# Softplus in a state-space layer: the predicated copy and VectorE's part in it taken out, the two branches added up by ScalarE and GpSimd

## What is computed

```python
xz = hidden_states @ in_proj_w.T
x, z = jnp.split(xz, 2, axis=-1)
x = silu(causal convolution of x with 4 taps)
dt, Bm, C = jnp.split(x @ x_proj_w.T, [16, 32], axis=-1)
dt = jax.nn.softplus(dt @ dt_proj_w.T + dt_proj_b)
def step(h, ins):
    dA = jnp.exp(dt_t[:, :, None] * A)
    h = dA * h + dt_t[:, :, None] * B_t[:, None, :] * x_t[:, :, None]
    y = jnp.einsum('bdn,bn->bd', h, C_t)
y = ys + x * D
return y * silu(z) @ out_proj_w.T
```

## Time and profile before

| | |
|---|---|
| Median of 3 runs | 3272.32 us (3270.14 to 3275.8) |
| Profiled execution, its own time | 3271.81 us |
| Its span, first to last instruction | 3270.1 us |
| Last stage | from about 2190 us to the end |
| DVE busy in 2190 to 3270 us | 977.99 us |
| PE, POOL, ACT busy in the same stretch | 946.28, 858.00, 509.88 us |

### The profile page before, as it was taken

The page is one execution under the profiler, slowest core; times in us unless marked ns, Lnnn a source line. Parts: engine busy times, 40 slices in busy tenths (PEclk is TensorE's granted clock), DMA queues, the critical chain, the costliest instruction groups (busy, mean ns, idle before and its releaser), DMA issues.

```text
span 3270.1 us, 45199 instructions
## 1 busy us (share of the span) xinstructions
PE 2865.6 (88%) x14018; PEld 1320.2 (40%) x14055; DVE 2167.0 (66%) x3006; ACT 1420.8 (43%) x2463; POOL 1267.8 (39%) x1424
## 2 busy tenths in 40 slices
PE   6895798988988989869999999678899899999986
PEld 5662133333332333236666666563222233223222
DVE  3577876866866767022222222564999999999997
ACT  2341055655655656812122211435445445545442
POOL 1143012112212212210000000744888888898885
PEclk9997588988999989979999999888899999998978
DMA  6166413133132220041111111740000000000000
GB/s 206 52 213 161 152 28 61 28 59 55 34 58 38 51 48 24 19 135 32 32 30 32 32 31 26 224 152 7 1 14 20 1 20 20 1 20 14 1 13 20
DMA packets 175061, 176.60 MB, mean 54 GB/s; under 512 B 50674, under 2 KB 151541, under 8 KB 174749
## 3 DMA queue, kind: packets, MB, share of 16 engines
q1 hardware_dynamic: 168732, 157.52, 18.9%
q0 software_dynamic: 6144, 16.82, 1.6%
HBM read 100.46 MB, written 73.83 MB: 53 GB/s over the span
## 4 chain that ended last, share of the span: by engine, by line
PE 54%; DVE 18%; POOL 10%; issue 9%; ACT 4%; DMA 3%; SPq 1%; POOLq 0%; DVEq 0%; ACTq 0%; PEldq 0%
PE ps L1679 50%; DVE hh L1645 6%; DVE mp L1421 6%; POOL Ch L907 5%; DVE ps L1632 2%; PE ps L1887 2%; POOL yg L806 2%; DMA ks<-qk_parts 1%; ACT Pt L1029 1%; DVE tl L1622 1%; DVE q L1333 1%; SPq L529 1%; PE ps L1843 1%; SPq L620 1%; ACT dA L1209 1%
## 5 line engine op out<-in xcount | busy, mean ns | idle before, releaser
L1421 DVE TENSOR_REDUCE mp<-ps 128x1 f32<-128x1024 f32 (+7 forms) x768 | 669.4, 909 | 245.3 <-PE ps L1679 234.2
L1029 ACT ACTIVATE Pt<-ps 128x512 f32<-128x512 f32 (+3 forms) x1280 | 609.2, 539 | 477.3 <-PE ps L1679 472.2
L907 POOL TENSOR_TENSOR Ch<-hh,Cb 128x1024 f32<-128x1024 f32 x256 | 603.1, 2358 | 41.0 <-DVE hh L1645 41.0
L1679 PE MATMUL ps<-ks,qs 96*128 96x512 bf16 (+3 forms) x1280 | 392.0, 379 | 96.2 <-DVE mp L1421 48.6
L1645 DVE TENSOR_TENSOR_SCAN hh<-dA,hst,ps 128x512 f32<-128x512 f32 x384 | 472.8, 1262 | 0.0
L767 POOL TENSOR_SCALAR_AFFINE_SELECT Pt<-Pt 128x128 f32<-128x128 f32 x512 | 146.8, 292 | 837.1 <-ACT Pt L1029 828.6
L1679 PE MATMUL ps<-qs,ks 99*128 99x512 bf16 (+3 forms) x1280 | 406.9, 365 | 16.0 <-ACT Pt L1029 15.6
L1209 ACT ACTIVATE dA<-ps 128x1024 f32<-128x1024 f32 x256 | 261.8, 1023 | 356.2 <-PE ps L1679 355.8
L1679 PE MATMUL ps<-dtx,pick 32*128 32x512 f32 x1024 | 324.8, 685 | 74.0 <-DVE hh L1645 73.1
L1632 DVE TENSOR_TENSOR ps<-ps,Bb 128x512 f32<-128x512 f32 x512 | 325.4, 680 | 28.0 <-PE ps L1679 27.7
L1679 PE MATMUL ps<-dt,WA 32*128 32x512 f32 x1024 | 321.1, 706 | 15.6 <-ACT dA L1209 14.6
(11 more groups left out here) (303 smaller groups left out, 3770.5 us busy)
## 6 DMA issues: line engine op xcount, KB each, us to landing
W<-in_L_ffn_w SPq DMA_DIRECT2D x16, 1024.0 KB, 12.1
qk_parts<-q SPq DMA_DIRECT2D x32, 384.0 KB, 2.9
qs<-qk_parts SPq DMA_DIRECT2D x96, 128.0 KB, 6.1
ks<-qk_parts SPq DMA_DIRECT2D x96, 128.0 KB, 7.8
expert_out<-yb SPq DMA_DIRECT2D x72, 128.5 KB, 2.6
...
```

The lines of the kernel that those rows point to most:

```text
L907: pool.tensor_tensor(Ch[:, k % 6, :, :], hh[:, k % HRING, :, :], Cb[:, par:par + 1, :].broadcast_to([P, 2, CH]), ALU.mult).then_inc(s_Ch, 1)
L1029: act.activation(Pt[:, n % PRING, q0:CH], ps[:, 4 + n % SRING, q0:CH], ACT.Exp, scale=SCALE).then_inc(s_exp, 1)
L1421: dve.tensor_reduce(mp[:, qc, h, t % TPC, k0 // 1024:k0 // 1024 + 1], slot[:, 0:n], AX.X, ALU.max).then_inc(s_free, 1)
L1679: return pe.matmul(o, lhsT, rhs, start=start, stop=stop, **kw)
```

## The change

Softplus' logarithm and its series are no longer chosen between; they are added. With a turning point t = 6 ln 2, ScalarE makes two exponentials: e1 = exp(-min(|v|, t)) (through a Relu of t - |v|), and e2 = exp(-max(|v|, t)) (through a Relu of |v| - t). The one that does not apply stays at the constant 2^-6. The result is max(v, 0) + ln(1 + e1) - ln(1 + 2^-6) + e2 * q(e2), where q is a quadratic that ScalarE makes with Square and Identity; `fix` holds the constants. For a block, ACT issues ten instructions where it issued five, POOL four where it issued six, and DVE none where it issued one. PE's queue is the same, instruction for instruction.

The function `series` and the functions `mask` and `select` are gone; `below_above` and `logarithm` are ACT's new ones, and `step_size` is POOL's, now in two steps.

```diff
-            def series(m, d, step):
...
-                    po.link(pool.tensor_scalar(p, t, 1.0 / 3, -0.5, ALU.mult, ALU.add))
-                    po.mark(pool.tensor_tensor(p, p, t, ALU.mult))
...
-                    po.link(pool.tensor_scalar(p, p, 1.0, 1.0, ALU.mult, ALU.add))
-                    pool.tensor_tensor(p, p, t, ALU.mult).then_inc(s_poly, 1)
...
-                pool.wait_ge(s_sel, b)
-                pool.tensor_tensor(dt[:, par, d, :], dt[:, par, d, :], tl[:, d, :], ALU.add).then_inc(s_dt, 1)
...
+            def step_size(m, d, step):
+
+                par, b = m % 2, m * KI + d + 1
+                x, q = dt[:, par, d, :], dtx[:, par, d, :]
                 if step == 0:
+                    pool.wait_ge(s_ln, b)
+                    po.mark(pool.tensor_tensor(x, x, tl[:, d, :], ALU.add))
+                    po.mark(pool.tensor_tensor(q, q, te[:, d, :], ALU.mult))
                 if step == 1:
                     po.settle()
+                    pool.tensor_tensor(x, x, q, ALU.add).then_inc(s_dt, 1)
+                    pool.wait_ge(s_dt, b)
+                    pool.wait_ge(s_xs, m + 1)
+                    pool.tensor_tensor(q, x, xs[:, par, d, :], ALU.mult).then_inc(s_dtx, 1)
...
-                if n == 0 and u in (5, 9, 13):
-                    step_size(0, u // 4)
-                if n + 1 < NC and u == 28:
-                    step_size(n + 1, 0)
-                if n and u in (0, 4, 8):
-                    step_size(n, u // 4 + 1)
...
+                if n == 0 and u in (2, 3, 7, 9, 13, 15):
+                    step_size(0, 1 + u // 6, u in (3, 9, 15))
                 if n + 1 < NC and u in (23, 25, 27, 29):
-                    series(n + 1, (u - 23) // 4, (u - 23) // 2 % 2)
-                if n + 1 < NC and u == 31:
-                    series(n + 1, 2, 0)
-                if n and u in (1, 3, 5):
-                    series(n, (2, 3, 3)[u // 2], (1, 0, 1)[u // 2])
+                    step_size(n + 1, (u - 23) // 4, (u - 23) // 2 % 2)
+                if n and u in (0, 4, 7, 9):
+                    step_size(n, 2 + u // 6, u in (4, 9))
...
                 ac.settle()
-                ac.link(act.activation(te[:, d, :], te[:, d, :], ACT.Exp, scale=-1.0))
-                act.activation(tl[:, d, :], te[:, d, :], ACT.Ln, bias=1.0).then_inc(s_ln, 1)
...
+            def below_above(m, d):
+
+                t, l = te[:, d, :], tl[:, d, :]
+                ac.mark(act.activation(l, t, ACT.Relu, bias=fix[:, 0:1], scale=-1.0))
+                ac.settle()
+                ac.mark(act.activation(t, t, ACT.Relu, bias=fix[:, 1:2]))
+                ac.settle()
+                ac.mark(act.activation(l, l, ACT.Exp, bias=fix[:, 1:2]))
+                ac.mark(act.activation(t, t, ACT.Exp, bias=fix[:, 1:2], scale=-1.0))
+                ac.settle()
+
+            def logarithm(m, d):
...
+                ac.mark(act.activation(l, l, ACT.Ln, bias=1.0))
+                ac.mark(act.activation(q, t, ACT.Square, bias=fix[:, 2:3], scale=1.0 / math.sqrt(3.0)))
+                ac.settle()
+                ac.mark(act.activation(l, l, ACT.Identity, bias=fix[:, 5:6]))
+                ac.mark(act.activation(q, q, ACT.Identity, bias=fix[:, 3:4]))
+                ac.settle()
+                act.sem_inc(s_ln, 1)
...
             take_BC(0, 1)
+            below_above(0, 0)
+            logarithm(0, 0)
             for d in range(1, KI):
                 take_dt(0, d)
-            mask(0, 0)
...
-                if n == 0 and u in (3, 7, 11):
-                    mask(0, u // 4 + 1)
-                if n and u in (2, 6):
-                    mask(n, u // 4 + 2)
+                if n == 0 and u in (0, 4, 7):
+                    below_above(0, (0, 4, 7).index(u) + 1)
+                if n == 0 and u in (1, 5, 9):
+                    logarithm(0, (1, 5, 9).index(u) + 1)
+                if n and u == 3:
+                    below_above(n, 3)
+                if n and u == 5:
+                    logarithm(n, 3)
...
-                if u in (26, 30):
-                    mask(n + 1, u // 4 - 6)
+                if u in (20, 24, 27):
+                    below_above(n + 1, (20, 24, 27).index(u))
+                if u in (21, 26, 29):
+                    logarithm(n + 1, (21, 26, 29).index(u))
...
-                dve.wait_ge(s_mask, m * KI + d + 1)
-                dve.copy_predicated(tl[:, d, :], te[:, d, :].bitcast(I32), dtx[:, m % 2, d, :]).then_inc(s_sel, 1)
...
-                if n == 0 and u in (5, 9, 13):
-                    select(0, u // 4)
-                if n + 1 < NC and u == 28:
-                    select(n + 1, 0)
-                if n and u in (0, 4, 8):
-                    select(n, u // 4 + 1)
```

More of the change, by code:

```diff
@@ L1132, in _ @@
             act.activation(A[:, :, :], A[:, :, :], ACT.Exp).then_inc(s_expA, 1)
+            act.wait_ge(s_none, 3)
+            ac.link(act.activation(fix[:, 6:7], fix[:, 4:5], ACT.Exp, bias=fix[:, 1:2]))
+            ac.link(act.activation(fix[:, 7:8], fix[:, 6:7], ACT.Ln, bias=1.0))
+            ac.link(act.activation(fix[:, 5:6], fix[:, 7:8], ACT.Copy, scale=-1.0))
             def take_x(m, d):
```

32 lines of the change are left out of this document (11 added, 21 removed).

## The result

The changed kernel took 3284.61 us in the median of six runs (3277.3 to 3289.16), the kernel before 3271.36 us on the same chip (3267.2 to 3275.8, six runs). The ratio is 1.0039, with a 95% interval of 1.0028 to 1.0049. I had forecast 3262 us and a range up to 3279. The profiled execution took 3277.3 us, its span 3275.5 us. It is the shortest of its six, but its last stage is 11.0 us longer than before, 1092.5 us against 1081.5.

The account below looks back on a forecast made before the run. DVE was taken as nearest to full in the last stage, with the dense chunk borders deciding. Borders 9.5, start -3.0 and chunk 0 3.6 gave 10 us off 3271.8; median forecast 3262 us, own range 3256 to 3267, with rivals 3240 to 3279.

Parts of the forecast that it names:

- The selects' price: At the seven chunk borders: removing DVE's selects wins 28.5 us if ACT is in time.
- ACT's groups: ACT's new instructions per block: `below_above` takes 2.82 us, `logarithm` 2.62, a dependent instruction 0.74.
- rival (4): Units 27 to 31: ACT becomes the bound if dependent instructions cost 0.2 us more; 3279 us, chance 0.15.
- rival 5: Last stage: POOL still ends last, so only select and series time on its chain goes, 5 us; 3267, chance 0.05.
- Step (c): Border 3/4 behind z3: a fixed sequence gives units 4 and 5 their spreads 10.7 and 15.0 us later; nothing won yet.
- Step (b): Border 3/4, units 27 to 31: ACT's groups delay PE 1.3 us, then half a microsecond; z3 ends 2.2 us later.
- Step (a): Border 3/4, from unit 20: ACT's groups put PE 2 us behind, won back in units 24 to 26, 0.6 behind at 27.
- the walk's delay for ACT: All seven borders: ACT's added work takes 19.0 us off the gain of 28.5, leaving 9.5.
- My own sign of being wrong: Borders 3/4 and 4/5: the prediction is wrong if they win more than 5 us or nothing.
- the last of the chances: Clock stretches falling elsewhere add a few microseconds to either side, within the range 3240 to 3279.
- Start: Start of the last stage: block 0's ACT groups ahead of the dt copies make z0 and the first spread 3.0 us later.
- Chunk 0: Chunk 0's three selects cost 0.8, 2.6 and 2.5 us; ACT's first group delays PE 2.3; 3.6 won.

Follow-up runs that it names:

- run 2: The kernel before with its 32 selects left out and nothing else changed: 0.9898 of the kernel before.
- run 8: The changed kernel with only block 0's ACT groups cut into pairs, in units 21 to 24, and some POOL steps moved: 1.0023 of the kernel before.
- run 9: The changed kernel with only blocks 1 to 3's ACT groups in pairs and later places, block 0's left: 0.9981 of the kernel before.
- run 4: The changed kernel with the spread of dt*x issued twice in units 22 and 23: 0.998 of the kernel before.
- run 6: The kernel before with the spread of dt*x issued twice in unit 22: 0.9984 of the kernel before.
- run 10: The changed kernel with the spread of dt*x issued twice in units 12 and 18 instead: 1.004 of the kernel before.
- run 12: The kernel before, unchanged, run once more for its trace: 3322.73 us, one execution.
- run 7: run 3 with repeated spreads in units 18 and 22, chunk 0's groups in pairs, and the start's groups behind the dt copies: 0.9925 of the kernel before.
- run 11: run 3 with the spread repeated in unit 22 and the start's ACT groups behind the dt copies: 0.9891 of the kernel before, 3283.54 us.
- second pair: One more execution each of the kernel before and the changed kernel, both unaltered, on other chips: last stage 1082.1 and 1095.3 us.
- run 3: The changed kernel with ACT's groups at the borders cut into pairs or moved to later units, POOL's steps behind them: 0.9935 of the kernel before.

## Why the prediction was wrong

**What held.** The selects' price as a sum: 28.5 us at the borders, 27.0 measured. ACT's groups: 2.82 and 2.62 us forecast, 2717.94 - 2715.06 = 2.88 and 2722.12 - 2719.34 = 2.78 in these rows of ACT in the changed kernel, with 0.75 us from one dependent instruction to the next where I took 0.74:

```profile
2715.06 0.73 ACT L1168 ACTIVATE tl<-te,fix 128x512 f32<-128x512 f32 x1
2715.82 0.72 ACT L1170 ACTIVATE te<-te,fix 128x512 f32<-128x512 f32 x1
2716.57 0.72 ACT L1172 ACTIVATE tl<-tl,fix 128x512 f32<-128x512 f32 x1
2717.20 0.71 ACT L1173 ACTIVATE te<-te,fix 128x512 f32<-128x512 f32 x1
2717.94 1.02 ACT L1217 ACTIVATE dA<-ps 128x1024 f32<-128x1024 f32 x1
...
2719.34 0.63 ACT L1181 ACTIVATE tl<-tl 128x512 f32<-128x512 f32 x1
...
2721.24 0.71 ACT L1185 ACTIVATE dtx<-dtx,fix 128x512 f32<-128x512 f32 x1
2722.12 1.02 ACT L1217 ACTIVATE dA<-ps 128x1024 f32<-128x1024 f32 x1 [0.17 <-ACT dtx L1185]
```

So rival (4) did not come about by its own condition, a dearer dependent instruction, although the result is on its side. POOL did not set the pace (rival 5): at every border its `Ch` of unit 0 starts 0.2 us or less behind DVE's unit, where before it was 3.2 to 7.1.

**Step (c), the fixed sequence behind z3, held to 0.1 us.** In the changed kernel z3 is made in the first row here:

```profile
2761.63 1.98 PE L1682 MATMUL ps<-xin,inw 128*128 128x512 f32 x4
...
2773.22 1.02 PE L1682 MATMUL ps<-dtx,pick 32*128 32x512 f32 x4
...
2778.01 0.59 PE L1682 MATMUL ps<-dtx,pick 32*128 32x512 f32 x2
```

It ends at 2763.61. The spreads for units 4 and 5 end at 2774.24 and 2778.60, 10.6 and 15.0 us later; the step said 10.7 and 15.0. DVE stands ready for both, and waits 1.53 and 0.84 us:

```profile
2774.29 1.30 DVE L1642 TENSOR_TENSOR ps<-ps,Bb 128x512 f32<-128x512 f32 x2 [1.53 <-PE ps L1682]
2775.50 2.32 DVE L1655 TENSOR_TENSOR_SCAN hh<-dA,ps 128x512 f32<-128x512 f32 x2
2778.66 1.30 DVE L1642 TENSOR_TENSOR ps<-ps,Bb 128x512 f32<-128x512 f32 x2 [0.84 <-PE ps L1682]
```

These waits are not ACT's doing alone: run 2, without its groups, has them too.

**Step (b) held in its sum, not in its parts.** PE's z3 ends 7.7 us behind DVE's unit 31 with the groups and 5.6 without (runs 8 and 9), 2.1 later where the step had 2.2. Units 0 to 8 show the same: ACT's groups cost 262.1 - 247.7 = 14.4 us there over all borders (run 4 against run 2), 2.06 a border. But the group in unit 27 makes PE wait 0.52 us in its unit 29 (run 4, at full clock, in the rows below), where the step had 1.3 a unit earlier.

**Step (a) failed.** It said that PE would be 2 us behind in unit 23, "wins it back in units 24 to 26, 0.6 behind at 27". The late spread came where it was forecast. But I costed units 24 to 26 at the full-clock pace of PE, in a stretch where the change had just put gaps of 0.48, 0.32 and 1.12 us in place of one of 1.56. The clock went to 1.2 GHz among them, PE won nothing back, and units 24 to 31 of the seven borders cost 244.9 - 216.2 = 29 us over run 2, where step (a) gives some 4 (7 x 0.6). With the repeats of run 4 they cost 219.9 - 216.2 = 3.7, and the borders are then 8.9 us better than before (482.0 against 490.9), where I had 9.5.

The step also left a group out. Block 1's `below_above` stands in unit 24, ahead of the `decay` that PE's unit 26 waits for, and the walk has no wait there. Run 4 shows it where units 24 to 31 have no half clock, at border 5/6: PE in its units 26 and 29, and DVE's `drive` of unit 30, up to whose spread PE does not idle again.

```profile
3031.66 1.13 PE L1682 MATMUL ps<-dt,WA 32*128 32x512 f32 x4 [1.31 <-ACT dA L1217]
...
3044.43 1.13 PE L1682 MATMUL ps<-dt,WA 32*128 32x512 f32 x4 [0.52 <-ACT dA L1217]
```

```profile
3040.97 1.30 DVE L1642 TENSOR_TENSOR ps<-ps,Bb 128x512 f32<-128x512 f32 x2 [1.17 <-PE ps L1682]
```

The wait of 1.3 us in unit 26 is there at six of run 4's seven borders.

That 8.9 comes so close to 9.5 flatters me. Run 4 has less half clock at its borders (54.4 us) than run 2 (92.7) and the kernel before (97.0), and the kernel before wins 9.5 us at its borders as well when it gets its own repeat (run 6, 481.4). With repeats in both kernels the change neither wins nor loses there, though even then run 6 has the more half clock (87.0 us). So the walk's delay for ACT was too small at full clock too. Borders of like clock give an estimate: where nothing or 3.4 us is at half clock, units 24 to 31 take 28.80 and 29.57 us before (4/5 and 3/4), and 30.36 and 31.13 in run 4 (5/6 and 2/3). That is 1.6 us a border or 11 in all; with the 14.4 of units 0 to 8 ACT's groups cost 25 us, where the walk had 19.0. Of the 24 us between forecast and result some 6 are then ACT's delay, 1.5 the selects' price, and the other 16 or so the clock.

My own sign of being wrong came with it: borders 3/4 and 4/5, forecast to win 3.1 and 2.8 us, lost 3.7 and 7.5.

The sentence that failed with it is the last of the chances, that clock stretches "that fall elsewhere add a few microseconds to either side". I had put the half clock at 0/1, 2/3 and 5/6 into the walk as given, like a property of these borders. Runs 4, 6 and 10 show that it answers to what PE did just before. The earlier trace rows held both parts: a gap of 1.56 us ahead of 2727.30, and behind it two matmuls in 1.22 us, where two take 0.70 at 2.4 GHz (2774.97). The Trainium skill ("TensorE: Matmul & The Clock Gate", section "A second HAM failure mode: psum-queue depth-cycling") says that many micro-idles of PE between groups of matmuls bring the clock down again and again. This trace agrees: gaps of 0.48 and 0.32 us, the fall to 0.50 granted at 2722.15, and then 2.08 us for matmuls that take 1.13. By that rule a case with more half clock at each border should have had a chance of its own; at run 12's 4.3 us for each of the three borders that I had walked as nearly free of it (1/2, 3/4, 4/5) it would have given 13 us more, 3275. The result lies 13 us above the kernel before, so that case too would have fallen short.

**Start.** Forecast 3.0 us later, measured 4.5. I let z0 wait for ACT's copy of dt2, which loses 4.2 us and wins 1.2 back. But PE's next projections wait for dt1's copy, which has nothing to win back yet:

```profile
2242.64 2.07 PE L1682 MATMUL ps<-xps,dtw 16*128 16x512 f32 x2 [7.37 <-ACT dt L1162]
2244.63 8.64 PE L1682 MATMUL ps<-xin,inw 128*128 128x512 f32 x16
```

z0 no longer waits for a copy, as it did in the earlier trace rows; it stands behind these two matmuls. In runs 7 and 11, with ACT's groups behind those copies, the first unit ends at 71.3 and 71.8 us, as before the change.

**Chunk 0.** Forecast 3.6 won, measured 6.2 (4.5 in the second pair). Run 2 divides it: without the selects and without ACT's groups chunk 0 takes 85.4 us, 7.2 less than before, where I had 5.9; ACT's groups then cost 1.0 (2.7 in the second pair), where I had 2.3. The selects' price was too small here; the delay lies within what two traces differ by.

**What stays open.** What makes the clock fall near unit 23 in the kernel before at four borders of seven and not at the others; why runs 8 and 9 leave the same half clock and still share out their gains between units 24 to 31 and 0 to 8; and how much of run 11's lead over run 3 is the repeat's and how much the start's beyond the 3.7 us that its first unit shows.
